# Halving the next expert's weights on other engines, a reordered front of the time mix, and one table set for logarithm and exponential

## The reference, cut to what matters

```
x = x + L0_attn(layernorm(x))   # delta rule with a fast and a slow state
x = x + L0_ffn(layernorm(x))    # 8 experts, the best 2 for each token
x = x + L1_attn(layernorm(x))   # RWKV time mix and channel mix
x = x + L1_ffn(layernorm(x))    # gated ternary feed-forward

# L0_ffn: h = gelu(x @ w1[e] + b1[e]);  y = h @ w2[e] + b2[e]
#         w1[e]: 256 x 1024, w2[e]: 1024 x 256, all fp32
# L1_attn, time mix: k, v, r = split(layernorm(x) @ W_tm), mixed with the previous token
#   per feature and step: ww = w + bb;  p = max(ww, k)
#   aa = exp(ww - p)*aa + exp(k - p)*v;  bb = p + log(exp(ww - p) + exp(k - p))
#   y = share of aa and v;  x = x + sigmoid(r)*y
```

## Time and profile before

| | us |
|---|---|
| median of three runs | 2255.67 |
| the profiled execution, its own time | 2259.32 |
| its span, first to last instruction | 2257.58 |
| PE busy (matmuls) | 1989.6 |
| DVE busy | 1389.7 |
| ACT busy | 968.1 |
| POOL busy | 321.2 |

### The profile page before, as it was taken

One profiled execution on the slowest core, in us unless ns is written; L12 is line 12 of the kernel. 1 busy time (PEld: TensorE's weight loads), 2 busy tenths in 40 slices (PEclk: granted clock), 3 DMA queues, 4 the chain that ended last, 5 costly groups with the idle time before them and its releaser, 6 DMA issues. The chain is left out here.

```text
span 2257.6 us, 32566 instructions
## 1 busy us (share of the span) xinstructions
PE 1989.6 (88%) x11554; PEld 1705.1 (76%) x11554; DVE 1389.7 (62%) x2744; ACT 968.1 (43%) x1776; POOL 321.2 (14%) x259
## 2 busy tenths in 40 slices
PE   8999999996488888889487638999899999999999
PEld 5799988985488888889455426777688888888887
DVE  7557666665566666666489977887353454454442
ACT  4655555542233332333488856664322322323221
POOL 0010012232444424442200000000000000000000
PEclk9999999995799999999788868999999999999999
DMA  3399111122334333232322231341300000000000
GB/s 98 119 369 401 38 46 55 55 72 98 99 75 96 75 75 75 43 66 43 107 66 56 75 84 56 112 151 54 122 17 3 19 19 0 19 19 0 19 10 11
DMA packets 86100, 170.36 MB, mean 75 GB/s; under 512 B 7216, under 2 KB 49840, under 8 KB 85808
## 3 DMA queue, kind: packets, MB, share of 16 engines
q1 hardware_dynamic: 65920, 132.47, 16.8%
q0 software_dynamic: 18176, 33.70, 7.7%
q10 hardware_dynamic: 1888, 2.67, 0.4%
HBM read 91.61 MB, written 88.74 MB: 80 GB/s over the span
## 5 line engine op out<-in xcount | busy, mean ns | idle before, releaser
L2632 ACT ACTIVATE x_tok<-bank,scl 128x512 f32<-128x512 f32 x128 | 88.3, 690 | 360.2 <-PE bank L2683 359.4
L2682 PE MATMUL bank<-hAh,ffn_h 128*128 128x512 f32 x512 | 202.7, 396 | 0.7 <-DVE x_tok L2560 0.7
L2682 PE MATMUL bank<-hBh,ffn_h 128*128 128x512 f32 x512 | 201.7, 394 | 0.0
L2683 PE MATMUL bank<-hAl,ffn_h 128*128 128x512 f32 x512 | 199.4, 389 | 0.0
L2683 PE MATMUL bank<-hBl,ffn_h 128*128 128x512 f32 x512 | 199.3, 389 | 0.0
L532 DVE TENSOR_TENSOR st<-st,bank 128x256 f32<-128x256 f32 x224 | 90.6, 418 | 112.3 <-PE bank L1157 95.0
L888 ACT ACTIVATE L<-bank 128x512 f32<-128x512 f32 x160 | 94.5, 595 | 147.6 <-PE bank L1150 141.8
L1476 POOL DMA_INDIRECT tokens_behind_spare_rows<-yg,row_of_token x72 | 112.1, 1557 | 311.1 <-DVE row_of_token L1630 290.9
L1563 ACT ACTIVATE yg<-yt,own_gates 128x256 f32<-128x256 f32 x70 | 31.9, 503 | 288.5 <-DVE yt L1625 281.8
L1570 ACT ACTIVATE h<-bank,b1s 128x256 f32<-128x256 f32 x280 | 126.1, 473 | 57.7 <-PE bank L1395 48.3
L1150 PE MATMUL bank<-L 128*128 128x128 f32 x768 | 147.8, 282 | 0.0
(11 more groups left out here) (439 smaller groups left out, 5659.4 us busy)
## 6 DMA issues: line engine op xcount, KB each, us to landing
z_by_expert<-zero SPq DMA_DIRECT2D x64, 520.0 KB, 16.0
st<-in_w_dram SPq DMA_DIRECT2D x14, 1024.0 KB
ckb<-in_ffn_dram POOLq DMA_DIRECT2D x32, 352.0 KB, 3.3
xg<-z_by_expert SPq DMA_DIRECT2D x36, 260.0 KB, 3.0
ffn_h<-ffn_copy SPq DMA_DIRECT2D x2, 4096.0 KB, 14.9
x_tok<-after_time_mix SPq DMA_DIRECT2D x15, 512.0 KB, 6.1
x_tok<-x_T SPq DMA_DIRECT2D x9, 512.0 KB, 4.3
tokens_behind_spare_rows<-x_tok SPq DMA_DIRECT2D x8, 512.0 KB
```

What stands on the lines that cost most here:

```text
L2632: A_.activation(gq[:, m % 4, :], B[2 + m % 4][:, :], ACT.Gelu, scale=scl[:, off[nm] + m:off[nm] + m + 1]).then_inc(g_act, 1)
L2682: T.matmul(out, w, x[0], start=first, stop=False)
L2683: return T.matmul(out, w, x[1], start=False, stop=last)
```

## The change

Five edits. (1) The split of experts 1 to 7 leaves POOL: at the first tile of expert e, ACT makes the high part of the next w1 ahead of the gelus and that of the next w2 behind them, once PE has raised `ex_done`, and DVE subtracts, w1 after `gate_of` and w2 at the end of its step. (2) Raw weights of odd experts get a place of their own in the token buffer `x_tok`, which is idle then; SP loads expert 1 there at once, ahead of its wait for the sorted rows, ACT issues expert 2, and SP then loads expert e+2 at expert e. (3) `down` waits for `w2_rdy` at every expert, `up` for `ew_rdy` as before. (4) In the front of the time mix DVE casts and subtracts the channel mix's weights itself (`channel_weights`), POOL doesn't, and `low_part(0)` comes ahead of `scales(1)`. (5) ACT loads the set that holds both logarithm and exponential, once before the first `root_logs` and at the top of every block.

```diff
+        raw1, raw2 = (st1, in_x_tok(0, KT, HID)), (st2, in_x_tok(KT * HID, KH, D))
+        nw_ld = [sem(f"next_weights_loaded_{q}") for q in range(2)]
+        def landed(e):
+            return nw_ld[e % 2], 32 * ((e + 1) // 2)
...
@@ SP, experts
             def weights(e):
-                sp.wait_ge(ew_free, e + 1)
-                sp.dma_start(st1[:, :, :], w1_d[e]).then_inc(ew_ld, 16)
-                sp.dma_start(st2[:, :, :], w2_d[e]).then_inc(ew_ld, 16)
+                if e >= 2:
+                    sp.wait_ge(ew_rdy, e - 1)
+                    sp.wait_ge(w2_rdy, e - 1)
+                sp.dma_start(raw1[e % 2][:, :, :], w1_d[e]).then_inc(nw_ld[e % 2], 16)
+                sp.dma_start(raw2[e % 2][:, :, :], w2_d[e]).then_inc(nw_ld[e % 2], 16)
...
+            sp.wait_ge(x1_st, 16 * NB)
+            weights(1)
             sp.wait_ge(scat, 16 * 2 * NC)
...
                 rows(e, t0, 0)
-                if 1 <= e < NE - 1:
-                    weights(e + 1)
+                if 1 <= e < NE - 2:
+                    weights(e + 2)
@@ POOL, experts
-            def split(e, q):
-                pool.wait_ge(ew_ld, e * 32 + 32)
-                pool.wait_ge(ex_done, e + 1)
-                for st_, w in ((st1, w1s[q]), (st2, w2s[q])):
-                    nc.gpsimd.tensor_copy(w[0][:, :, :], st_[:, :, :]).then_inc(p_st2, 1)
...
             def step(e, t, before, start):
                 add_to_tokens(t)
-                if before < e:
-                    if e + 1 < NE:
-                        split(e + 1, (e + 1) % 2)
-                    else:
-                        time_mix_weights()
+                if before < e and e == NE - 1:
+                    time_mix_weights()
@@ PE, experts
             def down(e, n):
-                if e == 0:
-                    pe.wait_ge(w2_rdy, 1)
+                pe.wait_ge(w2_rdy, e + 1)
@@ ACT, experts
+            def high_part(w, raw, e):
+                nc.scalar.activation(w[e % 2][0][:, :, :], raw[e % 2][:, :, :], ACT.Copy).then_inc(wh_rdy, 1)
+
             def step(e, t, before, start):
+                ahead = before < e and e + 1 < NE
+                if ahead:
+                    act.wait_ge(*landed(e + 1))
+                    high_part(w1s, raw1, e + 1)
                 for m in range(KH):
...
                     if start and m == 5:
-                        act.wait_ge(ew_free, 2)
-                        act.dma_start(st1[:, :, :], w1_d[1]).then_inc(ew_ld, 16)
-                        act.dma_start(st2[:, :, :], w2_d[1]).then_inc(ew_ld, 16)
+                        act.wait_ge(ew_rdy, 1)
+                        act.wait_ge(w2_rdy, 1)
+                        act.dma_start(st1[:, :, :], w1_d[2]).then_inc(nw_ld[0], 16)
+                        act.dma_start(st2[:, :, :], w2_d[2]).then_inc(nw_ld[0], 16)
+                if ahead:
+                    act.wait_ge(ex_done, e + 2)
+                    high_part(w2s, raw2, e + 1)
                 if not start:
                     gated(t)
@@ DVE, experts
+            def low_part(w, raw, e, wanted, done):
+                dve.wait_ge(wh_rdy, wanted)
+                hi, lo = w[e % 2]
+                V.tensor_tensor(lo[:, :, :], raw[e % 2][:, :, :], f32(hi[:, :, :]), ALU.subtract).then_inc(done, 1)
+
             def step(e, t, before, start):
+                ahead = before < e and e + 1 < NE
                 gate_of(e, t)
+                if ahead:
+                    low_part(w1s, raw1, e + 1, 2 * e + 3, ew_rdy)
                 rows_split(t + 1)
...
                 hand_on(t)
+                if ahead:
+                    low_part(w2s, raw2, e + 1, 2 * e + 4, w2_rdy)
@@ POOL, time mix
-            high_weights(0)
-            high_weights(1)
             for b in range(NB):
                 add_to_sum(b)
@@ DVE, time mix
-            def low_weights(n):
-                dve.wait_ge(cw_hi, n + 1)
+            def channel_weights(n):
+                dve.wait_ge(cw_ld[n], 16)
                 w = (wcm, wcp)[n]
                 hi, lo = (a[:, :, :].rearrange("p k n -> p (k n)") for a in w)
+                V.tensor_copy(hi, cst[n]).then_inc(cw_hi, 1)
+                dve.wait_ge(cw_hi, n + 1)
                 V.tensor_tensor(lo, cst[n], f32(hi), ALU.subtract).then_inc(cw_rdy, 1)
...
             scales(0)
             variances(1)
+            channel_weights(0)
+            low_part(0)
             scales(1)
-            low_part(0)
-            low_weights(0)
             variances(2)
+            channel_weights(1)
             exponents(0)
-            low_weights(1)
             scales(2)
             low_part(1)
@@ ACT, time mix
             diagonals()
+            nc.scalar.preload_act_table_set(LOG_EXP)
             root_logs(0)
...
             for b in range(NB):
+                nc.scalar.preload_act_table_set(LOG_EXP)
                 if b + 1 < NB:
                     columns(b + 1)
                 logs(b)
```

More of the change, by code:

```diff
@@ L28 @@
 MIN_TILES = 2
+LOG_EXP = "natural_log_exp_and_others"
 ZW = D + 4
@@ L1378, in build @@
         wt_ld = sem("w_tm_loaded")
-        ew_free, ew_rdy, ex_done = (sem("expert_stage_free"), sem("expert_weights_split"), sem("expert_done"))
+        raw1, raw2 = (st1, in_x_tok(0, KT, HID)), (st2, in_x_tok(KT * HID, KH, D))
+        nw_ld = [sem(f"next_weights_loaded_{q}") for q in range(2)]
+        def landed(e):
+            return nw_ld[e % 2], 32 * ((e + 1) // 2)
+        ew_rdy, ex_done = sem("w1_split"), sem("expert_done")
         eb_ld, xg_ld, xt_ps, xT_rdy = (sem("expert_biases_loaded"), sem("rows_loaded"), sem("rows_T_in_psum"),
@@ L1387, in build @@
         turn_seen = sem("scatter_turns_seen")
-        wh_rdy, w2_rdy = sem("first_weights_high"), sem("first_w2_split")
+        wh_rdy, w2_rdy = sem("weights_high"), sem("w2_split")
         p_st2, x_st, h_st = sem("weights_hi_done"), sem("rows_hi_done"), sem("h_hi_done")
@@ L1433, in _ @@
                 rows(e, t0, 0)
-                if 1 <= e < NE - 1:
-                    weights(e + 1)
+                if 1 <= e < NE - 2:
+                    weights(e + 2)
                 if e == 2:
-                    sp.wait_ge(x1_st, 16 * NB)
                     sp.dma_start(wst, A["W_tm"].rearrange("(k p) n -> p k n", p=128)).then_inc(wt_ld, 16)
@@ L1468, in time_mix_weights @@
                     nc.gpsimd.tensor_tensor(wst[:, k, :], wst[:, k, :], tmr_, ALU.mult).then_inc(p_st2, 1)
-                pool.wait_ge(p_st2, (NE - 1) * 2 + KT)
+                pool.wait_ge(p_st2, KT)
             def add_to_tokens(n):
@@ L1591, in _ @@
             dve.sem_inc(dn_ps, 2)
-            dve.sem_inc(ew_free, 1)
             dve.sem_inc(rg_tk, 1)
@@ L1658, in _ @@
             V.tensor_tensor(w2s[0][1][:, :, :], st2[:, :, :], f32(w2s[0][0][:, :, :]), ALU.subtract).then_inc(w2_rdy, 1)
-            dve.wait_ge(w2_rdy, 1)
-            dve.wait_ge(ew_rdy, 1)
-            dve.sem_inc(ew_free, 1)
             expert_tiles(dve, step)
@@ L1780, in _ @@
             P = nc.gpsimd
-            def high_weights(n):
-                pool.wait_ge(cw_ld[n], 16)
-                P.tensor_copy((wcm, wcp)[n][0][:, :, :].rearrange("p k n -> p (k n)"), cst[n]).then_inc(cw_hi, 1)
             def add_to_sum(b):
```

## The result

The changed kernel takes 2181.86 us (median of four runs, 2177.72 to 2187.91) against 2256.74 us before (four runs): ratio 0.9671, 95% interval 0.9644 to 0.9699. That is 74.9 us less, 1.1 us under the low end of the range given and 14.8 us more than the forecast of -60.1. Its profiled execution, the fastest of the four, took 2177.72 us with a span of 2175.9.

A forecast was written before the change was run, and what follows sets the result against it. It took POOL's splits holding DVE and starving PE as the experts' bound, DVE as the time mix's. -58.5 + 5 + 2 - 8.6 + 0 = -60.1 us gave 2195 us on the median's scale; range 2183 to 2213.

The forecast's parts named there:

- The base: Experts' stage: time over 31 ordinary tile periods of 11.88 us, 77.6 us in all, to go with POOL's splits.
- the last switch: Switch to the last expert, where POOL's multiply of W_tm stays and holds a DVE copy: 1.7 us of the surplus kept.
- what the change puts back at a switch: Six expert switches: PE waits of 1.65 and 0.6 us plus a drain of 0.6, 17.4 us, before any lost clock.
- the wait at m=4: Switch step of `up`: ACT's cast of w1 makes gelu m=0 late, so PE waits 1.65 us, once per switch.
- The wait behind the cast of w2: Step after a switch: ACT's cast of w2 delays its next gelu m=0, so PE waits 0.6 us.
- The clock: PE's half clock behind the new waits at six switches: half of 1.7 us each, +5 us, bounds 0 to 10.
- rival A: Half clock for 7 to 10 us behind each of six switches, a term of 21 to 30 us; chance 0.09.
- The start: Before the first rows: expert 1's 2 MB issued ahead of them delays their landing, +2 us, bounds 0 to 4.5.
- The front: Start of the time mix: POOL's casts gone and low_part(0) earlier start PE's first products sooner, -8.6 us, bounds -5 to -9.
- The table set: Time mix blocks: one of three table loads of 1.28 us goes on ACT; 0 us, bounds -3 to +1.
- the case that the experts gain all: Experts' stage: no clock term, no start cost, casts covered by early y; 2183 to 2188 us, chance 0.08.
- Slower: Whole kernel slower than before, if PE's clock stays low between switches: 2256 to 2280 us, chance 0.03.

The follow-up runs named there:

- the double cast: The changed kernel with ACT's cast of w1 made twice at switches 1 to 6: 2206.36 us, ratio 0.9772 to the kernel before.

## Why the prediction was wrong

**The bound was read rightly.** POOL's splits hold DVE, and PE starves two engines further on. Shown by leaving them out: -76.9 us in the experts.

**The base was 4.6 us too small.** My "31 periods at 11.88" gave 77.6 gross and, less 3.6 of drains and 1.7 of the last switch, 72.3 for the splits; they were worth 76.9. The 1.7 had no place in the sum: the last expert's switch begins with the scatter at 1046.91, where the 31 periods end, and its period is 14.27 us before, after and without splits. Of the 3.6 only 2.05 is there, since the 31 periods without splits sum to 370.33 us against 368.28: the drains are partly made up by the first period, which is 9.63 us without a split, not 11.88. The last 1.4 lie ahead of the first scatter, a stretch of 17.1 to 18.7 us over the profiles, and may be chance.

**The step that failed: what the change puts back at a switch.** It was written as 6 x (1.65 + 0.6) of waits and "+5 us, half" for the clock, 18.5 us; the chip says 9.9. Its terms: (1) the wait at m=4 was right in mechanism and place, 1.35 for 1.65, 8.2 us over six switches; no run takes the other 1.7 apart. (2) The wait behind the cast of w2, 0.6, is nil: I let ACT go at PE's restart, but ACT's cast, released by `ex_done`, started 0.44 us ahead of that restart, and its gelu m=0 was ready at 927.6, before PE wanted it. (3) The clock was nil. I took the middle of two bounds where the case had to be on one side, since all six switches have the same wait. The row that I used for the upper bound (0.52 over 288 to 291 us) stands behind a wait of about the same length, 1.40 us, but in the first stage, with other waits around it, while the experts' matmuls are end to end; whether that is the reason no run tests. The trace of before had a much nearer row, which I missed: at 596.03, in expert 0's first tiles, PE waits 1.66 us for its rows, just the length that I forecast, and the clock over 592 to 611 us is 1.00.

```profile
596.03 0.39 PE L1393 MATMUL bank<-xTh,w_0h 128*128 128x256 f32 x1 [1.66 <-DVE xTl L1618]
...
592.00:611.00 19.00, 16.94 (x142) 16.51 (x141) 14.04 (x21) 5.51 (x12) 9.58 (x5) 1.00 0.55 154
```

That clock can cost something at these very switches, where the wait is 3.3 us, is shown by the double cast: rival A was a true mechanism at twice the wait, and at 13 us over six switches cheaper than its 21 to 30.

**The start** was +2 and is +3.4, and +3.8 by moving the load. The cost is real, but its mechanism was wrong, so that the size is near is luck. The prediction let the rows queue behind expert 1's weights, and cited the rule that would put them there (rows can't pass weights in one ring, +4.5). In the changed kernel the rows' load was issued as the weights were through, and PE had the rows 2.6 to 3.0 us after the issue in all fourteen profiles. Late were POOL's scatters of the first stage, for which SP waits ahead of that load (the trace has no landing of theirs, so this is read from SP's wait): 4.1 to 4.4 us from the issue of the last one to the load of rows in the eight kernels without the weights in flight, 7.8 to 8.7 in the six with them. So this load says nothing for or against the rule.

**The front** was -8.6 and is -7.7. a3h came 2.4 us sooner rather than 3.1, and the cover of 1.6 us over DVE's new work was used up: the second block's tokens landed late (a wait of 1.96 us) and the subtract ended as a3h came. The cast itself took 1.22 us for my 1.3.

**The table set** was 0 in the sum, and nothing in the loop speaks against it, though the reason I gave covers only a part. "DVE is full" is right of the loop; in the front two loads were on the path, and the rows after the change show no wait for them ahead of the low part, which the reorder put first. No run has the whole change without the set.

**The range.** The touched stretches sum to -71.4 and the medians to -72.8 and -74.9. With base and switch right and the other terms as forecast the same working gives -76.9 + 9.9 + 2 - 8.6 = -73.6, or 2182.1, which is itself under the range: its low end of 2183 was built on the base of 72.3. I had placed the case that the experts gain all at 2183 to 2188 and given it 0.08. Of its three conditions only one came true, that the clock costs nothing; the time came out at its end because the base was larger. Slower, at 0.03, had nothing for it.

## What to carry to other kernels

When one engine is seen late in a regular loop, measure the beat and sum the surplus; then look on which engine a common instruction takes several times its usual length, for that is where the loss enters, however far from the engine that waits. Work moved to another engine is priced by its slack ahead of the next due event, not by its share of busy time: the same cast costs 1.5 us a switch ahead of the gelus (8.8 us over six) and next to nothing behind them. Here a term of the clock was on or off for all like waits, so decide it by the row that is most like the new wait and its surroundings, and don't halve it. A load that is moved ahead of a wait can delay what that wait is for, on another engine's queue too: look at when the next load is issued, and not only at how long it takes.

## What the runs showed of the hardware

The hold goes both ways. Where DVE's two-input subtract of 2.29 us runs, POOL's indirect DMA takes 3.26 or 3.05 us to issue instead of 1.55 (914.90 and 915.36, 927.60 and 928.26 above), and both issues end 1.4 us behind the subtract's end. It costs nothing that the trace shows, since the next tile's scatter is 10 us off. The Trainium skill ("SBUF — State Buffer", section on the two separate sides) says that DVE and GpSimd share one pair of ports under an exclusive lock, held for a whole instruction, and that a DVE operation with two SBUF inputs takes it only against a GpSimd operation that reads SBUF. The trace agrees as far as the indirect DMA's issue counts as such a reader, which the section doesn't say: it names descriptors as held up by DVE's two-port modes. By the measurement the subtract holds them up too; which part of the issue is held no run separates.

DMAs of one engine's queue delay those of another's. With 2 MB of weights in flight from SP's queue, SP's wait for POOL's scatters ended 7.8 to 8.7 us after the issue of the last one, and 4.1 to 4.4 us after it without.

The clock: at waits of 1.33 to 1.42 us in six places, and of 1.66 in one more, none of TensorE's clock was lost; at waits of 3.3 and 5.3 us half clock came every time and lasted 3.4 or 6.8 us, and at the 8.2 us of the kernel before 6.8 or 10.2, which there begins within the wait, so that 2.9 to 6.2 of it fall behind it. Where between 1.66 and 3.3 us it begins in this loop stays open.

The same first stage ended between 549 and 569 us over the fourteen profiles, on several chips, so differences of single profiles are to be taken stretch by stretch.
